# One transfer instead of two for the row of maxima of two attention heads, with both heads' low parts of Q in the same 64 partitions

## Chip, cores and metric

The kernel runs on one core of one Trainium2 chip. The metric is the device time of one execution in microseconds; the time given is the median of several executions. The profile is one execution recorded by the hardware profiler.

## The reference

The input x has 4 sequences of 1024 tokens with 128 features, all in float32. Four lines carry what matters here: attention over 16 heads of 64 features, with a causal mask and a softmax, and a layer norm behind it.

```
q, k, v = einsum('BSE,EHK->BSHK', x, w_q / w_k / w_v)          # 16 heads, K = 64
probs   = softmax(q k / sqrt(64) + causal mask, over the keys)
x       = layernorm(x + einsum('BSHK,EHK->BSE', probs v, w_o))
x       = layernorm(x + ffn(x))     # 128 -> 512, butterflies, gelu, butterflies, 512 -> 128
```

The softmax subtracts the maximum of each row of scores. The kernel must do this too, or get the same value in another way.

## The kernel before, in words

The attention is cut into 32 units (`UNITS`): 4 sequences times 8 pairs of heads. Each unit has 12 steps (`STEPS`); a step is one block of 128 keys against one chunk of up to 512 queries, and it is done for both heads of the pair.

**How a score is made.** TensorE works in fp32r, so Q and K are split in a high part (rounded) and a low part (the rest). A score is made by two matmuls into the same PSUM bank, in `scores`. The first (L671) multiplies `KHL` by `QH`: for head 0 the lower 64 partitions (0 to 63) of `KHL` hold K's high part and the upper 64 (64 to 127) its low part, and `QH` holds Q's high part in both halves; for head 1 the halves of `KHL` are swapped. The second (L675) multiplies `KH1` by `QL`. For head 0 the lower half of `KH1` holds a copy of K's high part and its upper half ones; the lower half of `QL` holds Q's low part, and its upper half zeros but for one row, partition 64 (`K`), which holds the negated maximum of each query. For head 1 it is the other way round: copy and low part above, ones and the row of maxima below, the row in partition 0. So the second matmul adds the low part's product and subtracts the maximum in one go, and ScalarE then only takes the exponential (L841).

**Where the row of maxima comes from.** During unit u, TensorE also does the work of unit u + 1 in the gaps ("fillers", laid out by hand in `FILL`): projections of Q and K (`proj`, L597 to L599), projections of V, and for the maxima the scores once more in one pass (`max`, L621). VectorE takes the maximum of each row (L966, L969) and then of the parts (L973). The last step of the chain is the filler `mt`, at step 10 between the two heads: TensorE transposes the maxima (L626), VectorE copies them to `NROW`, 16 rows of 128 numbers, 8 rows for each head (L979), and SyncE sends them to the rows of `QL` (`rows`, L392), with one transfer of 4 KB for each head. Each adds 16 to the semaphore `m_landed`. The second matmul of step 0, head 0, of the next unit (L675) waits until both have landed:

```
                    if s == 0 and h == 0:
                        pe.wait_ge(m_landed, (unit + 1) * 32)
```

**What else touches these tiles.** ScalarE rounds Q and K out of PSUM (`evacuate`, L778), one instruction for each head. VectorE subtracts the rounded part to make the low part (`lo`, L890, called in `consume`). SyncE copies Q's high part to the other half of `QH` (L378), and K's high part from `KHL` to `KH1` (L382), one transfer for each head and chunk; `dup_landed` counts them, and the first `max` filler of each chunk waits for it. `QL` is double-buffered (`par`), so a row of unit u + 1 goes to another buffer than the one that unit u reads. The zeros of `QL` are set once by VectorE (L893, L894), the ones of `KH1` once by GpSimd (L453, L455).

**The order on SyncE's queue.** In each unit: the copies of the next unit (`copies`), the three transfers of the inverted sums of the unit before (`inverses`), then the rows (`rows`), and in some units one 512 KB load of butterfly weights (`stage_weights`, L360). SyncE waits in this order, so nothing overtakes.

Of the kernel before, what the change touches and what calls it, by code (L numbers as in the profile page):

```python
# [24 lines left out]
F32 = mybir.dt.float32  # L25
# [3 lines left out]
P = 128  # L29
B, S, D = 4, 1024, 128  # L30
H, K = 16, 64
# [157 lines left out]
def post_norm_layer(nc, x, w_q, w_k, w_v, w_o, W_exp, b_exp, up_w, up_b, down_w, W_con, b_con, down_b, out):  # L189
    ctx = ExitStack()  # L190
    with ctx:
# [153 lines left out]
        @block.sync  # L345
        def _(sp):
            sp.dma_start(X[:, 0:TILES, :], x_tiles[:, 0:TILES, :]).then_inc(in_x[0], 16)
            for n, w in enumerate((w_q, w_k, w_v)):
                sp.dma_start(WQKV[:, n, :], w.rearrange("e h k -> e (h k)")).then_inc(in_w, 16)
            sp.dma_start(BLOCKS, b_exp.rearrange("(a n) -> a n", a=HT)).then_inc(in_b, 16)  # L350
            sp.dma_start(up_b_row, up_b.rearrange("(a n) -> a n", a=1)).then_inc(in_b, 16)
            sp.dma_start(W1[:, :], W_exp).then_inc(in_exp, 16)

            def stage_weights(n):

                if n > 0:
                    sp.wait_ge(composed, 3 * n)
                w, st = (up_w, n) if n < STAGES else (down_w, 2 * STAGES - 1 - n)
                src = w[st:st + 1].rearrange("a k i o -> a (k i o)").broadcast_to([P, 2 * HID])
                sp.dma_start(SW[:, :], src).then_inc(stage_in, 16)  # L360

            for st in range(STAGES):
                w = up_w[st:st + 1].rearrange("s k i o -> s (k i o)")
                if st < BLOCK_STAGES:
                    sp.dma_start(inner_w[st], w.rearrange("s (a n) -> (s a) n", a=HT)).then_inc(in_rows, 16)
                else:
                    sp.dma_start(outer_w[st - BLOCK_STAGES], w).then_inc(in_rows, 16)
            sp.dma_start(X[:, TILES:, :], x_tiles[:, TILES:, :]).then_inc(in_x[1], 16)

            def copies(unit):  # L370

                par = unit % 2
                A, Bh = slice(0, K), slice(K, P)
                for c in range(CHUNKS):
                    cols = slice(c * CH, (c + 1) * CH)
                    sp.wait_ge(qk_hi, (unit * 2 * CHUNKS + (2 * c + 1)))
                    for h, src, dst in ((0, A, Bh), (1, Bh, A)):
                        sp.dma_start(QH[dst, par, h, cols].bitcast(F32), QH[src, par, h, cols].bitcast(F32))\  # L378
                            .then_inc(dup_landed[c], 16)
                    sp.wait_ge(qk_hi, (unit * 2 * CHUNKS + (2 * c + 2)))  # L380
                    for h, half in ((0, A), (1, Bh)):
                        sp.dma_start(KH1[half, par, h, cols].bitcast(F32), KHL[half, par, h, cols].bitcast(F32))\  # L382
                            .then_inc(dup_landed[c], 16)

            def rows(unit):

                par = unit % 2
                sp.wait_ge(nrow_made, (unit + 1))
                for h in range(2):
                    row = K if h == 0 else 0  # L390
                    dst = QL[row:row + 1, par, h, :].rearrange("a (t c) -> a t c", t=TILES)
                    sp.dma_start(dst.bitcast(F32), NROW[h * TILES:(h + 1) * TILES, :].bitcast(F32)).then_inc(m_landed, 16)  # L392


            def inverses(unit):

                sp.wait_ge(sums_out, unit + 1)
                sp.dma_start(RCOL[:, 0, :], R0[0:P:P // 4, :].rearrange("a (p e) -> a p e", p=P // 4)).then_inc(sums_landed, 16)
                sp.wait_ge(recip_made, unit + 1)
                sp.wait_ge(o_free, unit * CHUNKS + O_CREDIT)  # L400
                sp.dma_start(RROW.rearrange("h (p e) -> (h p) e", p=K), RCOL[:, 1, :]).then_inc(recip_landed, 16)
                sp.wait_ge(recip_landed, unit * 16 + 16)
                for h in range(2):
                    sp.dma_start(R[h * K:(h + 1) * K, :, :].rearrange("p q c -> p (q c)"),
                                 RROW[h:h + 1, :].broadcast_to([K, CHUNKS * CH])).then_inc(inverse_landed, 16)

            copies(0)
            sp.sem_inc(sums_landed, 16)
            sp.wait_ge(blocks_done, 1)
            sp.dma_start(BROW, BLOCKS).then_inc(brow_in, 16)  # L410
            sp.dma_start(wo_nat, w_o.rearrange("e h k -> e (h k)")).then_inc(in_wo, 16)
            sp.dma_start(wcon_nat, W_con.rearrange("(t p) d -> p t d", p=P)).then_inc(in_con, 16)
            sp.dma_start(BC[:, :], b_con.rearrange("(a n) -> a n", a=1).broadcast_to([P, D])).then_inc(in_bc, 16)
            sp.dma_start(down_row, down_b.rearrange("(a n) -> a n", a=1).broadcast_to([P, D])).then_inc(in_bc, 16)
            rows(0)
            for u in range(UNITS):
                if u + 1 < UNITS:
                    copies(u + 1)
                if u > 0:
                    inverses(u - 1)  # L420
                if u + 1 < UNITS:
                    rows(u + 1)
                for n in range(2 * STAGES):
                    if STAGE_UNIT[n] - 1 == u:
                        stage_weights(n)
            inverses(UNITS - 1)
            sp.wait_ge(m_landed, 32 * UNITS)
            for c in range(CHUNKS):
                sp.wait_ge(dup_landed[c], 64 * UNITS)

            for g in range(B * CHUNKS):
                sp.wait_ge(out_made, (g + 1) * TPC)
                sp.dma_start(out_tiles[:, g * TPC:(g + 1) * TPC, :],
                             X[:, g * TPC:(g + 1) * TPC, :]).then_inc(out_stored, 16)
            sp.wait_ge(out_stored, 16 * B * CHUNKS)
# [3 lines left out]
        def _(pool):  # L439
# [10 lines left out]
            nc.gpsimd.memset(HALF[:], -0.5).then_inc(half_set, 1)  # L450

            pool.wait_ge(half_set, 1)
            nc.gpsimd.memset(KH1[K:P, :, 0, :].bitcast(F32), 1.0).then_inc(ones_rows_set, 1)  # L453
            pool.wait_ge(ones_rows_set, 1)
            nc.gpsimd.memset(KH1[0:K, :, 1, :].bitcast(F32), 1.0).then_inc(ones_rows_set, 1)  # L455
            pool.wait_ge(ones_rows_set, 2)
            pool.sem_inc(add_done, ADD_CREDIT)
            pool_n = 2

# [96 lines left out]
        def _(pe):  # L556
# [105 lines left out]
            def scores(unit, s):  # L662
                qc, kt = STEPS[s]
                par = unit % 2
                q0, n = qc * CH + START[s], CH - START[s]
                for h in range(2):
                    use = 2 * s + h
                    dst = SC[use % NSC][:, 0:n]

                    pe.wait_ge(exp_done, unit * 2 * NS + use + 1)  # L670
                    nc.tensor.matmul(dst, KHL[:, par, h, kt * P:(kt + 1) * P], QH[:, par, h, q0:q0 + n],  # L671
                                     start=True, stop=False)
                    if s == 0 and h == 0:
                        pe.wait_ge(m_landed, (unit + 1) * 32)
                    nc.tensor.matmul(dst, KH1[:, par, h, kt * P:(kt + 1) * P], QL[:, par, h, q0:q0 + n],  # L675
                                     start=False, stop=True).then_inc(scores_ready, 1)
                    if h == 0:
                        fill(unit, s, BETWEEN)
# [42 lines left out]
                t = nc.tensor.matmul(lay_banks[len(LAY) % 4][:, i:i + 1], BROW[:, i * P:(i + 1) * P], ONES[0:1, 0:1],  # L721
                                     start=True, stop=True)
            t.then_inc(laid_made, 1)
            pe.wait_ge(ones_rows_set, 2)
            pe.wait_ge(laid_copied, len(LAY) + 1)
            for u in range(UNITS):
                window(u)
# [152 lines left out]
        def _(dve):  # L880
# [8 lines left out]
            def lo(dst, src, hi_part):  # L889
                return nc.vector.tensor_tensor(dst, src, hi_part.bitcast(F32), ALU.subtract)  # L890


            nc.vector.memset(QL[K:P, :, 0, :].bitcast(F32), 0.0)  # L893
            nc.vector.memset(QL[0:K, :, 1, :].bitcast(F32), 0.0)  # L894
            nc.vector.memset(NEGM[:], 0.0)
            nc.vector.memset(MP[:], LOWEST).then_inc(rows_set, 1)

# [37 lines left out]
            def consume(u, f, at):  # L935
# [3 lines left out]
                if f[0] == "proj":  # L939
# [7 lines left out]
                    A, Bh = slice(0, K), slice(K, P)  # L947
                    if n == 0:
                        lo(QL[A, nxt, 0, cols], w[A, :], QH[A, nxt, 0, cols])
                        op = lo(QL[Bh, nxt, 1, cols], w[Bh, :], QH[Bh, nxt, 1, cols])  # L950
                    else:
                        lo(KHL[Bh, nxt, 0, cols], w[A, :], KHL[A, nxt, 0, cols])
                        op = lo(KHL[A, nxt, 1, cols], w[Bh, :], KHL[Bh, nxt, 1, cols])
# [21 lines left out]
                elif f[0] == "mt":  # L975
                    dve.wait_ge(work_ready, at + 1)
                    if u >= 0:
                        dve.wait_ge(m_landed, (u + 1) * 32)
                    nc.vector.tensor_copy(NROW[:, :], w[0:2 * TILES, 0:P]).then_inc(nrow_made, 1)  # L979
                    dve.wait_ge(nrow_made, u + 2)  # L980
                    dve.sem_inc(free, 1)
# [160 lines left out]
```

## Time and profile before

| | us |
|---|---|
| median of 3 executions | 1057.71 |
| lowest and highest | 1055.47, 1058.67 |
| the profiled execution, its own time | 1057.07 |
| its span, first to last instruction | 1054.7 |

In the profile PE is TensorE's matmuls, PEld its weight loads, DVE VectorE, ACT ScalarE, POOL GpSimd and SPq the queue of SyncE that issues transfers. L675 is line 675 of the kernel. Matmuls are pipelined, and their ends are modelled; two matmul rows may overlap. A wait is inferred from the semaphores: the profile names the engine or transfer that came last. Times in the timeline count from the start of the span.

### The profile page before, as it was taken

The page shows a single profiled execution, that of the slowest core. Times are in us where ns is not written, and L with a number is a line of the kernel's source. Part 1 is how long each engine was busy: PE and PEld are TensorE (multiplying, and loading weights), DVE is VectorE, ACT ScalarE, POOL GpSimd, SP SyncE. Part 2 cuts the span into 40 slices and gives each one's busy share as a digit, 9 for nine tenths or more (in the row PEclk, how much of TensorE's full clock was granted, in tenths as well). Part 3 has the DMA queues.
Part 4 walks back from the last instruction along what each step waited for, and adds up shares of the span by engine and source line. Part 5 has one row for each costly group of instructions (what it writes and reads, how often), then busy time and mean ns, then how long its engine had stood idle before and what let it go on. Part 6 is the DMA issues. An engine that isn't in the chain of part 4 may idle for free.

```text
span 1054.7 us, 17699 instructions
## 1 busy us (share of the span) xinstructions
PE 1016.9 (96%) x5816; PEld 697.3 (66%) x5816; DVE 754.2 (72%) x2014; ACT 602.9 (57%) x1214; POOL 757.4 (72%) x726
## 2 busy tenths in 40 slices
PE   4799999999999999999999999999999999999997
PEld 3556666676666666767666766766666676675576
DVE  6666777777677778777778777776778778873456
ACT  4355566665565566666656556666656656664431
POOL 6278776777779777777779877777778987777322
PEclk9699999999999999999999999999999999999998
DMA  7112223232231223232231222332222222320002
GB/s 221 45 46 66 56 57 82 62 81 75 48 81 38 65 62 82 62 81 62 62 81 47 66 53 61 81 81 62 72 52 81 63 51 53 80 62 21 21 18 64
DMA packets 45800, 68.69 MB, mean 65 GB/s; under 512 B 15079, under 2 KB 21515, under 8 KB 45710
## 3 DMA queue, kind: packets, MB, share of 16 engines
q1 hardware_dynamic: 45710, 67.57, 25.2%
q8 instruction: 47, 0.77, 0.3%
q14 instruction: 43, 0.35, 0.1%
HBM read 31.11 MB, written 2.36 MB: 32 GB/s over the span
## 4 chain that ended last, share of the span: by engine, by line
PE 86%; DMA 6%; POOL 3%; DVE 2%; issue 2%; SPq 1%; ACT 0%; POOLq 0%; DVEq 0%; ACTq 0%
PE O L696 24%; PE WORK L621 13%; PE SC L671 12%; PE SC L675 12%; PE WORK L636 4%; PE WORK L658 3%; PE WORK L758 3%; PE WORK L599 3%; PE WORK L598 3%; PE WORK L597 3%; DMA QL<-NROW 2%; DMA R<-RROW 2%; PE SC L746 1%; PE WORK L746 1%; PE WORK L607 1%
## 5 line engine op out<-in xcount | busy, mean ns | idle before, releaser
L841 ACT ACTIVATE PR<-SC 128x512 f32<-128x512 f32 (+3 forms) x768 | 355.0, 490 | 283.4 <-PE SC L675 247.3
L498 POOL TENSOR_TENSOR SUM<-SUM,PR 128x1024 f32<-128x1024 f32 (+3 forms) x256 | 419.1, 1637 | 14.0
L966 DVE CUSTOM_DVE_ANT_0 WORK<-WORK,CMASK 128x128 f32<-128x128 f32 (+3 forms) x512 | 239.4, 514 | 65.0 <-PE WORK L621 65.0
L671 PE MATMUL SC<-QH,KHL 128*128 128x512 f32 (+3 forms) x768 | 272.0, 359 | 4.8 <-ACT PR L841 3.2
L675 PE MATMUL SC<-QL,KH 128*128 128x512 f32 (+3 forms) x768 | 263.9, 347 | 3.1 <-DMA QL<-NROW 3.0
L483 POOL TENSOR_SCALAR_AFFINE_SELECT PR<-PR 128x256 f32<-128x256 f32 x256 | 105.7, 414 | 213.1 <-ACT PR L841 212.9
L621 PE MATMUL WORK<-KHL,QH 128*128 128x512 f32 (+3 forms) x768 | 224.8, 361 | 5.1 <-DMA KH<-KHL 3.7
L696 PE MATMUL O<-PR,VLO 128*64 128x512 f32 (+3 forms) x1024 | 200.0, 522 | 2.0 <-DVE OT L1036 1.9
L671 PEld LDWEIGHTS SC<-QH,KHL 128*128 128x128 f32 x768 | 145.3, 189 | 63.3 <-ACT PR L841 29.2
L621 PEld LDWEIGHTS WORK<-KHL,QH 128*128 128x128 f32 x768 | 135.5, 190 | 55.8 <-issue 34.9
L969 DVE TENSOR_REDUCE MP<-WORK 128x1 f32<-128x512 f32 x256 | 164.3, 685 | 4.6
L675 PEld LDWEIGHTS SC<-QL,KH 128*128 128x128 f32 x768 | 145.5, 189 | 16.3 <-DMA QL<-NROW 5.9
L890 DVE TENSOR_TENSOR QL<-WORK,QH 64x512 fp32r<-64x512 f32 x128 | 88.1, 688 | 78.6 <-ACT QH L778 77.6
L507 POOL TENSOR_TENSOR SUM<-PR 128x768 f32<-128x768 f32 x64 | 136.3, 2130 | 1.4 <-ACT PR L841 1.4
L696 PEld LDWEIGHTS O<-PR,VLO 128*64 128x64 f32 x1024 | 64.9, 136 | 106.3 <-issue 78.4
L890 DVE TENSOR_TENSOR KHL<-WORK,KHL 64x512 fp32r<-64x512 f32 x128 | 88.1, 688 | 43.2 <-ACT KHL L778 41.1
L778 ACT ACTIVATE QH<-WORK 64x512 fp32r<-64x512 f32 x128 | 75.6, 590 | 28.6 <-PE WORK L599 27.8
L778 ACT ACTIVATE KHL<-WORK 64x512 fp32r<-64x512 f32 x128 | 75.9, 593 | 4.7 <-PE WORK L599 1.4
L696 PE MATMUL O<-PR,VHI 128*64 128x256 f32 (+3 forms) x512 | 74.3, 432 | 0.0
L966 DVE DVE_READ_ACCUMULATOR2_ANT MP<- 128x1 f32 x512 | 72.7, 142 | 0.0
L696 PEld LDWEIGHTS O<-PR,VHI 128*64 128x64 f32 x512 | 36.8, 137 | 52.6 <-issue 46.8
L636 PE MATMUL WORK<-WOT,OT 128*128 128x128 f32 x512 | 63.7, 278 | 0.0
(102 smaller groups left out, 1070.9 us busy)
## 6 DMA issues: line engine op xcount, KB each, us to landing
QH<-QH SPq DMA_DIRECT2D x128, 128.0 KB, 2.3
KH<-KHL SPq DMA_DIRECT2D x128, 128.0 KB, 2.3
R<-RROW SPq DMA_DIRECT2D x64, 256.0 KB, 3.9
SW<-in_L_ffn_up_weights_dram SPq DMA_DIRECT2D x9, 512.0 KB, 4.7
SW<-_L_ffn_down_weights_dram SPq DMA_DIRECT2D x9, 512.0 KB, 4.8
out_dram<-X SPq DMA_DIRECT2D x8, 256.0 KB, 2.3
QL<-NROW SPq DMA_DIRECT2D x64, 4.0 KB
X<-in_L_attn_x_BSE_dram SPq DMA_DIRECT2D x1, 512.0 KB, 4.3
```

The costliest lines, as they stand in the source:

```text
L498: nc.gpsimd.tensor_tensor(total, total, prob(unit, s), ALU.add).then_inc(add_done, 1)
L507: nc.gpsimd.tensor_tensor(total, first[:, :, START[s]:], prob(unit, s), ALU.add).then_inc(add_done, 1)
L621: t = nc.tensor.matmul(w[:, at_col:at_col + n], QH[:, nxt, h, qt * P:(qt + 1) * P], KHL[:, nxt, h, lo:lo + n], start=True, stop=True)
L636: t = nc.tensor.matmul(w[:, k * P:(k + 1) * P], attended(pair, qc)[:, k * P:(k + 1) * P], WOT[:, pair % PAIRS, :], start=pair < last, stop ...
L671: nc.tensor.matmul(dst, KHL[:, par, h, kt * P:(kt + 1) * P], QH[:, par, h, q0:q0 + n], start=True, stop=False)
L675: nc.tensor.matmul(dst, KH1[:, par, h, kt * P:(kt + 1) * P], QL[:, par, h, q0:q0 + n], start=False, stop=True).then_inc(scores_ready, 1)
L696: t = nc.tensor.matmul(O[qc][h * K:(h + 1) * K, START[s]:], values(unit, kt)[:, h * K:(h + 1) * K], p[:, h, :], start=kt == 0, stop=s == L ...
L778: return nc.scalar.activation(dst, src, ACT.Copy)
L841: nc.scalar.activation(prob(unit, s)[:, h, :], SC[use % NSC][:, 0:n], ACT.Exp, scale=K ** -0.5).then_inc(exp_done, 1)
L890: return nc.vector.tensor_tensor(dst, src, hi_part.bitcast(F32), ALU.subtract)
L966: op = nc.vector.tensor_tensor_reduce(cols, cols, CMASK[:, CH - n:], 1.0, LOWEST, ALU.add, ALU.max, cell)
L969: op = nc.vector.tensor_reduce(cell, cols, AX_X, ALU.max)
```

## The change

Both heads now have the same layout in the second matmul: the low part of Q and the copy of K's high part lie in partitions 0 to 63, ones and the row of maxima in partitions 64 to 127, the row in partition 64. Both rows then lie one behind the other in one partition, and one transfer of 8 KB carries both. VectorE's subtraction for head 1 reads partitions 64 to 127 and writes 0 to 63; SyncE's copy of K's high part for head 1 goes from the upper to the lower half.

```diff
                     for h, half in ((0, A), (1, Bh)):
-                        sp.dma_start(KH1[half, par, h, cols].bitcast(F32), KHL[half, par, h, cols].bitcast(F32))\
+                        sp.dma_start(KH1[A, par, h, cols].bitcast(F32), KHL[half, par, h, cols].bitcast(F32))\
                             .then_inc(dup_landed[c], 16)
...
                 sp.wait_ge(nrow_made, (unit + 1))
-                for h in range(2):
-                    row = K if h == 0 else 0
-                    dst = QL[row:row + 1, par, h, :].rearrange("a (t c) -> a t c", t=TILES)
-                    sp.dma_start(dst.bitcast(F32), NROW[h * TILES:(h + 1) * TILES, :].bitcast(F32)).then_inc(m_landed, 16)
-
+                dst = QL[K:K + 1, par, :, :].rearrange("a h (t c) -> a (h t) c", t=TILES)
+                sp.dma_start(dst.bitcast(F32), NROW[:, :].bitcast(F32)).then_inc(m_landed, 16)
...
-            nc.gpsimd.memset(KH1[K:P, :, 0, :].bitcast(F32), 1.0).then_inc(ones_rows_set, 1)
+            nc.gpsimd.memset(KH1[K:P, :, :, :].bitcast(F32), 1.0).then_inc(ones_rows_set, 1)
             pool.wait_ge(ones_rows_set, 1)
-            nc.gpsimd.memset(KH1[0:K, :, 1, :].bitcast(F32), 1.0).then_inc(ones_rows_set, 1)
-            pool.wait_ge(ones_rows_set, 2)
...
                     if s == 0 and h == 0:
-                        pe.wait_ge(m_landed, (unit + 1) * 32)
+                        pe.wait_ge(m_landed, (unit + 1) * 16)
...
-            nc.vector.memset(QL[K:P, :, 0, :].bitcast(F32), 0.0)
-            nc.vector.memset(QL[0:K, :, 1, :].bitcast(F32), 0.0)
+            nc.vector.memset(QL[K:P, :, :, :].bitcast(F32), 0.0)
...
                         lo(QL[A, nxt, 0, cols], w[A, :], QH[A, nxt, 0, cols])
-                        op = lo(QL[Bh, nxt, 1, cols], w[Bh, :], QH[Bh, nxt, 1, cols])
+                        op = lo(QL[A, nxt, 1, cols], w[Bh, :], QH[Bh, nxt, 1, cols])
...
                     if u >= 0:
-                        dve.wait_ge(m_landed, (u + 1) * 32)
+                        dve.wait_ge(m_landed, (u + 1) * 16)
```

The other waits on `m_landed` (SyncE's at the end) and on `ones_rows_set` (TensorE's before the first unit) count 16 and 1 in place of 32 and 2.

## Rows read from the trace of the kernel before

**Rows 1.** The page: busy time of each engine.
```profile
PE 1016.9 (96%) x5816; PEld 697.3 (66%) x5816; DVE 754.2 (72%) x2014; ACT 602.9 (57%) x1214; POOL 757.4 (72%) x726
```
**Rows 2.** The chain of waits that ended last, by engine (the page).
```profile
PE 86%; DMA 6%; POOL 3%; DVE 2%; issue 2%; SPq 1%; ACT 0%; POOLq 0%; DVEq 0%; ACTq 0%
```
**Rows 3.** Waits over the whole span: who waited for what, us in total, times, longest.
```profile
PEld SC L675 <- DMA QL<-NROW: 5.9, 9, 1.3
...
PE SC L675 <- DMA QL<-NROW: 3.0, 6, 0.9
```
**Rows 4.** Timeline at a boundary of units without a wait (start, length, what).
```profile
275.13 1.43 SPq L392 DMA_DIRECT2D QL<-NROW  x2
...
276.98 1.18 SPq L378 DMA_DIRECT2D QH<-QH  x2
...
277.80 0.19 PEld L675 LDWEIGHTS SC<-QL,KH 128*128 128x128 f32 x1
```
**Rows 5.** Chain in order of time at a boundary with a wait.
```profile
334.07 0.70 SPq L392
334.82 3.10 DMA QL<-NROW
337.97 0.51 PE SC L675
```
**Rows 6.** Windows of two units in turn: length, busy times, PEclk, DMA share, GB/s.
```profile
304.70:334.05 29.35, 29.35 (x173) 20.19 (x172) 22.53 (x64) 18.18 (x38) 22.00 (x21) 1.00 0.27 73
334.05:364.54 30.49, 29.66 (x173) 20.18 (x172) 22.72 (x65) 18.38 (x39) 24.02 (x23) 1.00 0.23 54
```
**Rows 7.** Timeline: the three longest of the nine waiting weight loads (bracket: idle before).
```profile
161.29 0.19 PEld L675 LDWEIGHTS SC<-QL,KH 128*128 128x128 f32 x1 [1.25 <-DMA QL<-NROW]
...
337.96 0.19 PEld L675 LDWEIGHTS SC<-QL,KH 128*128 128x128 f32 x1 [1.15 <-DMA QL<-NROW]
...
721.01 0.19 PEld L675 LDWEIGHTS SC<-QL,KH 128*128 128x128 f32 x1 [0.69 <-DMA QL<-NROW]
```
**Rows 8.** Transfers between 277 and 278 us, in 40 slices of 0.025 us.
```profile
GB/s 0 0 0 0 0 0 0 0 82 42 41 0 0 0 0 0 0 0 0 0 0 0 0 0 0 0 0 0 0 0 0 0 0 0 0 0 0 0 0 0
```
**Rows 9.** Transfers between 335 and 337 us, in 40 slices of 0.05 us, and by queue.
```profile
GB/s 0 0 0 0 0 0 0 0 389 11 0 0 0 0 0 0 0 0 0 0 0 0 31 31 10 0 0 0 0 0 10 10 0 0 0 0 0 0 0 0
...
q8 instruction: 1, 0.02, 3.5%
```
**Rows 10.** Transfers between 571.5 and 573 us, in 40 slices of 0.0375 us, and by queue.
```profile
GB/s 0 0 0 0 0 0 0 0 0 0 0 0 55 55 437 0 0 0 0 0 0 0 0 0 0 0 0 0 0 0 0 14 68 28 0 0 0 0 0 0
...
q8 instruction: 1, 0.02, 3.9%
```
**Rows 11.** Timeline: the weight load that follows the transfers of rows 10.
```profile
573.29 0.19 PEld L675 LDWEIGHTS SC<-QL,KH 128*128 128x128 f32 x1
```
**Rows 12.** Groups by line: busy, mean ns of one, idle before.
```profile
L890 DVE TENSOR_TENSOR QL<-WORK,QH 64x512 fp32r<-64x512 f32 x128 | 88.1, 688 | 78.6 <-ACT QH L778 77.6
L890 DVE TENSOR_TENSOR KHL<-WORK,KHL 64x512 fp32r<-64x512 f32 x128 | 88.1, 688 | 43.2 <-ACT KHL L778 41.1
```
**Rows 13.** Issues of transfers: count, KB, median us to landing (the page).
```profile
QH<-QH SPq DMA_DIRECT2D x128, 128.0 KB, 2.3
KH<-KHL SPq DMA_DIRECT2D x128, 128.0 KB, 2.3
R<-RROW SPq DMA_DIRECT2D x64, 256.0 KB, 3.9
```
**Rows 14.** Timeline from the issue of K's copies to the first maxima of the next unit.
```profile
280.84 1.10 SPq L382 DMA_DIRECT2D KH<-KHL  x2
...
285.74 0.30 PEld L621 LDWEIGHTS WORK<-KHL,QH 128*128 128x128 f32 x2 [0.84 <-issue]
```
**Rows 15.** Timeline of the start: the first row and the first unit.
```profile
38.14 1.34 SPq L392 DMA_DIRECT2D QL<-NROW  x2
...
42.36 0.77 PE L671 MATMUL SC<-QH,KHL 128*128 128x512 f32 x1 [1.48 <-issue]
```

More of the change, by code:

```diff
@@ L426, in _ @@
             inverses(UNITS - 1)
-            sp.wait_ge(m_landed, 32 * UNITS)
+            sp.wait_ge(m_landed, 16 * UNITS)
             for c in range(CHUNKS):
@@ L723, in _ @@
             t.then_inc(laid_made, 1)
-            pe.wait_ge(ones_rows_set, 2)
+            pe.wait_ge(ones_rows_set, 1)
             pe.wait_ge(laid_copied, len(LAY) + 1)
```

## The prediction

> **What bounds the kernel now.** The page comes first: TensorE is busy 96% of the span, no other engine over 72% [rows 1]. The chain of waits says the same, PE 86% and DMA 6% [rows 2]. So only what gives TensorE time back counts. The waits over the whole span then say where it stands still: the weight load of the second matmul waited for the row of maxima 9 times, 5.9 us in all, 1.3 us at most. The matmul behind it shows 6 such waits, 3.0 us, which are the same stalls seen a second time and are not added [rows 3].
>
> There are 32 boundaries of units, and only 9 wait. The timeline shows why. At an ordinary one the two transfers are issued from 275.13 us on, in 1.43 us, and the weight load that needs them starts at 277.80 with no idle before it [rows 4]. So the row is there at most 2.67 us after the issue. When did it move? Between 277 and 278 us the bytes of the second transfer show at 277.20 to 277.27 [rows 8]: 2.07 us after the first issue. It landed between 2.07 and 2.67 us after it. The slack is between nothing and 0.60 us.
>
> At a boundary with a wait the first issue is at 334.07, the second at 334.82, and the matmul goes on at 337.97: the row took 3.10 us from the second issue, 3.85 from the first [rows 5]. In that stretch a 16 KB packet of the instruction queue starts in the same slice as the row's packets, 335.40, and a last piece of the row moves only from 336.50 on, when the others moved at 336.10 to 336.25 [rows 9]. My reading is that the fetch of instructions sits before one piece of the row in one DMA engine. It doesn't always hit: at 572.05 such a packet starts with the row's, the second set moves on time at 572.7, and the load at 573.29 has no wait [rows 10, 11].
>
> Does a wait lengthen the kernel by its full size? The unit with the wait of 1.15 us [rows 7] lasts 30.49 us, the one before it, with as many matmuls, 29.35 [rows 6]: 1.14 longer. Nothing downstream absorbs it. So the 5.9 us are the whole sum to be had.
>
> **The change part by part.**
> *The second issue goes.* The first transfer's issue takes 0.70 us and the second starts 0.75 after the first [rows 5]. One transfer carries all 16 rows of NROW, so the full row lands 0.75 us earlier if a transfer takes as long from its own issue: between 1.32 and 1.92 us after the issue. The slack grows to between 0.75 and 1.35 us. A delay that made a wait of up to 0.75 us now makes none. Of the nine, two are longer, 1.25 and 1.15 us; the third longest is 0.69 [rows 7]. The other seven, 5.9 - 1.25 - 1.15 = 3.5 us, vanish. The two leave 0.50 + 0.40 = 0.90 us, if the same fetch hits one transfer as it hit two; if the row is through before the fetch comes (it is out 0.75 earlier), they leave nothing. The gain is 5.0 to 5.9 us; I take the middle, 5.4.
>
> *Length of the issue and of the flight.* The bytes double in one transfer, 4 to 8 KB, all into one partition. The nearest rows bound the flight: the copies of 128 KB land 2.3 us after their issue, R's 256 KB 3.9 us [rows 13]. In the rows of before, 8 packets were moved within three slices of 0.025 us [rows 8], so 16 cost some 0.1 us more at most if they queue at one partition; I take 0 to 0.1, and the slack of 0.75 covers it. The issue may be a little cheaper: a pair of K's copies takes 1.10 us [rows 14] against 1.43 for a pair of rows [rows 4], 0.16 for one. Neither enters the sum, since an ordinary boundary has slack.
>
> The Trainium skill (DMA: Bandwidth & Descriptors, "Why a DMA increments its semaphore by 16 and not by 1") says that a transfer runs on the largest number of engines up to 16 that divides the slowest dimension of both sides: 8 for each of the old ones, 16 for the new, and that it counts as landed when all have finished. By that rule a fetch on any engine can hold up the row, where before half of them couldn't. The sum above would keep part of the waits; that is the first rival.
>
> *SyncE's queue.* It is free 0.7 us sooner behind the rows. Behind them stand the next copies of Q, issued at 276.98, 0.42 us after the rows' issue ended at 276.56 [rows 4]: they wait for ScalarE, not for the queue. Gain nothing. In the units with the 512 KB load, this starts earlier; it stood behind the rows before too.
>
> *VectorE.* The low part of Q of head 1 is now written across halves. The same instruction already crosses halves for K's low part: 688 ns for both, 64x512 each [rows 12]. Nothing, 0 to 0.
>
> *K's copy of head 1 crosses halves*, and both copies now write the lower one. The pair is issued from 280.84 on, in 1.10 us, so the second at about 281.39, and first used at 285.74 [rows 14]. With the 2.3 us to landing of both kinds of copy [rows 13] it is there at 283.7, 2.0 us early. Only if it took twice as long, 4.6 us, would it be late, by 0.3 us. Q's copies cross halves already, in both directions, and land in the same 2.3 us, so I take nothing.
>
> *Matmuls.* Same shapes, same counts, same number of zeros and ones. Nothing. *Memsets and start.* Two fills become one of the same size, on VectorE and on GpSimd, in the first microseconds; the first row, issued at 38.14 us, is needed only behind 42.36 [rows 15], so the start has slack for a later row too. Nothing. VectorE's `mt` waits for a transfer of a whole unit ago. Nothing.
>
> **Sum.** -5.4 us on the profiled execution: 1057.07 - 5.4 = 1051.7. The median shown is 0.64 above that execution, which gives 1052.3; between the two I say 1052.0. A measurement of this kernel can tell about 0.3%, 3.2 us, from no change, so the gain is a little above what can be seen.
>
> **The rivals.**
> *The fetch still hits.* With the row spread over more engines, other fetches get in its way. For it: all nine waits are tails, and the packet that missed at 572.05 may have been on an engine that the row didn't use. Against: only delays over 0.75 us still cost. If all nine became as long as the longest, each would leave 0.50: 4.5 us, a gain of 1.4, 1056.3. Same.
> *The time is given back.* TensorE comes earlier, and another engine is late at the boundary, or a fetch falls onto the copies instead. Against it is the comparison of two units above. Half the gain, 2.7 us: 1055.0, on the border.
> *Slower.* The single transfer lands later than the two did, in every unit: split over fewer engines because the two heads stay a dimension of two, or its 16 pieces queue at one partition. This would also be the change not doing what it says. It decides from 2.67 us after the issue [rows 4]; every 0.1 us beyond costs 32 x 0.1 = 3.2 us. At 2.9 us it is 7.4 us slower with the nine waits kept, 1065; as late as R's 3.9 [rows 13] it would be 39. Against it: the destination is one row without gaps, and 8 KB is a sixteenth of what lands in 2.3 us.
>
> **How the numbers follow.** The forecast has 0.65, the fetch 0.17, given back 0.12, slower 0.06. Faster by over 0.3%: the forecast and half of the third, 0.71; within 0.3%: 0.23; slower 0.06. The range reaches from the lowest run less the full 5.9 (1055.47 - 5.9 = 1049.6) to the first rival at 1056.3; it leaves out the slower case and some spread between executions.
>
> **What would show it.** One issue of rows in each unit, some 0.6 to 0.7 us; 32 in all. No wait of the second matmul's weight load for the row, or one or two under 0.6 us; units of 29.1 to 29.4 us where 30.49 stood. The prediction is wrong if these waits still sum to over 2 us, or if they are gone and the span hasn't shrunk by 4 us.

## The result, and the profile after

The changed kernel takes 1050.66 us (median of 9 executions, 1050.25 to 1052.58); the kernel before, measured with it, 1056.84 us (9 executions, 1054.45 to 1058.67). The ratio is 0.9935, with a 95% interval of 0.9922 to 0.9948: some 6.9 us less, between 5.5 and 8.2 (the two medians are 6.2 us apart). The profiled execution took 1050.42 us with a span of 1048.5, 6.2 us less than the span of before.

From the page of the kernel after, the line of busy times and that of the chain by engine:

```profile
PE 1014.8 (97%) x5816; PEld 697.7 (67%) x5816; DVE 753.1 (72%) x2013; ACT 602.8 (57%) x1214; POOL 757.2 (72%) x725
...
PE 91%; DMA 3%; DVE 2%; POOL 2%; issue 1%; SPq 1%; ACT 0%; POOLq 0%; DVEq 0%; ACTq 0%
```

TensorE has the same 5816 matmuls [rows 1], in a shorter span. In the chain the transfers' share went from 6% [rows 2] to 3%, and TensorE took it over: the row's transfer, 2% of the chain before by the page, is in it no more.

The view of the line that issues the row (L390, which was L392), kernel after. Its columns are the shortest, median and longest issue in ns, and the first and last start; then who waited for it, and the time from the start of an issue to landing:

```profile
L390 SPq DMA_DIRECT2D QL<-NROW x32: 547/552/575, 38.2 to 945.8; - x32
its engine sat idle before it (us, times) until:
who waited for it (us, times):
busy tenths in 40 slices 0000000000000000000000000000000000000000
DMA to landing us min/median/max: 1.8/1.8/1.8
```

Two things are to be seen. Nobody waited for the row, in any of the 32 units, where before there were 9 waits of 5.9 us in all [rows 3]. And the row never landed later than 1.8 us after its issue, where the longest of before needed nearly 4 from the first issue. The need is where it was at nearly all boundaries: 2.66 us after the issue. Here is the timeline of the kernel after at the boundary that stands in [rows 5], which lost 1.15 us before:

```profile
332.20 0.55 SPq L390 DMA_DIRECT2D QL<-NROW  x1
...
334.05 1.15 SPq L378 DMA_DIRECT2D QH<-QH  x2
334.75 0.19 PEld L666 LDWEIGHTS SC<-QH,KHL 128*128 128x128 f32 x1
...
334.86 0.19 PEld L670 LDWEIGHTS SC<-QL,KH 128*128 128x128 f32 x1
```

The last weight load starts 2.66 us after the issue (334.86 - 332.20), with no idle in a bracket. The windows of the two units that answer to [rows 6]:

```profile
302.85:332.20 29.35, 29.35 (x173) 20.16 (x172) 22.41 (x64) 18.17 (x38) 22.01 (x21) 1.00 0.27 73
332.20:361.57 29.37, 29.37 (x173) 20.20 (x172) 22.68 (x65) 18.36 (x39) 24.05 (x23) 1.00 0.23 56
```

The second was 30.49 us long and is 29.37: the 1.15 us of the wait, less 0.03, are back. The other lines that the change touches are as they were: the subtractions 688 ns for `QL` and 689 for `KHL`, K's copies 2.3 us to landing, each memset one of 3.5 us in place of two of 1.8.

### The profile page after: what moved, and what is told of

Its sections match the earlier page's. It is cut to its first block, busy times and chain, and to the rows that moved or that the text cites. A ratio compares the mean times of both kernels' runs of the same rounds, so it can differ in the third digit from the quotient of the medians.

```text
span 1048.5 us, 17665 instructions
## 1 busy us (share of the span) xinstructions
PE 1014.8 (97%) x5816; PEld 697.7 (67%) x5816; DVE 753.1 (72%) x2013; ACT 602.8 (57%) x1214; POOL 757.2 (72%) x725
## 3 DMA queue, kind: packets, MB, share of 16 engines
HBM read 31.11 MB, written 2.36 MB: 32 GB/s over the span
## 4 chain that ended last, share of the span: by engine, by line
PE 91%; DMA 3%; DVE 2%; POOL 2%; issue 1%; SPq 1%; ACT 0%; POOLq 0%; DVEq 0%; ACTq 0%
PE O L691 25%; PE WORK L616 14%; PE SC L666 13%; PE SC L670 12%; PE WORK L631 5%; PE WORK L653 3%; PE WORK L753 3%; PE WORK L594 3%; PE WORK L592 3%; PE WORK L593 3%; PE WORK L602 1%; PE WORK L604 1%; PE WORK L603 1%; PE SC L741 1%; PE WORK L741 1%; DMA R<-RROW 1%
```

## Experiments

Four questions were put. Does the gain come from the layout or from the transfer? Is it a matter of when the row lands against 2.66 us? Does the number of rows (and so of engines) in a transfer matter? Is it the delay or the extra traffic? The times below are ratios to the kernel before on the same chip. The kernels of the first four share one measurement, those of the last four another; in both the kernel before was at 1059 us.

### The new layout with two transfers

```diff
-                dst = QL[K:K + 1, par, :, :].rearrange("a h (t c) -> a (h t) c", t=TILES)
-                sp.dma_start(dst.bitcast(F32), NROW[:, :].bitcast(F32)).then_inc(m_landed, 16)
+                for h in range(2):
+                    dst = QL[K:K + 1, par, h, :].rearrange("a (t c) -> a t c", t=TILES)
+                    sp.dma_start(dst.bitcast(F32), NROW[h * TILES:(h + 1) * TILES, :].bitcast(F32)).then_inc(m_landed, 16)
```

The waits on `m_landed` count 32 for each unit again.

> The kernel after with its new layout, but with two transfers of 8 rows again, both into partition 64. Theory (the moment at which the whole row has landed is all that counts): two issues 0.75 us apart, the row whole at about 2.54 us after the first issue, against a need at 2.66; some 9 waits of the second matmul's weight load for the row, 4 to 7 us, and the time of the kernel before, 1056 to 1057.5 us. Rival 1 (the gain comes from the layout, the copies and subtractions that all go to the lower half): the gain stays, 1050 to 1052 us.

Measured: ratio 1.0001 (0.9986 to 1.0017), span 1053.9. The waits in its profile, us in total, times, longest:

```profile
PEld SC L671 <- DMA QL<-NROW: 5.4, 9, 1.3
```

Nine waits and 5.4 us, as before. Layout, subtractions, copies and memsets together are worth nothing that can be measured (the interval is some 1.6 us to either side). The whole gain is in how the row is sent.

### The old kernel with a semaphore for each head's row

```diff
-                    sp.dma_start(dst.bitcast(F32), NROW[h * TILES:(h + 1) * TILES, :].bitcast(F32)).then_inc(m_landed, 16)
+                    sp.dma_start(dst.bitcast(F32), NROW[h * TILES:(h + 1) * TILES, :].bitcast(F32)).then_inc(m_landed[h], 16)
...
-                    if s == 0 and h == 0:
-                        pe.wait_ge(m_landed, (unit + 1) * 32)
+                    if s == 0:
+                        pe.wait_ge(m_landed[h], (unit + 1) * 16)
```

VectorE and SyncE wait for both where they waited for 32.

> The kernel before, layout and both transfers unchanged, but each row has a semaphore of its own, and head 1's second matmul waits for head 1's row, head 0's only for its own. Theory: head 0's row lands 0.7 us before it is needed, head 1's is needed a good 0.46 us later than before (two matmuls of 0.23 us). Of the nine waits only their parts over 0.46 us stay: 0.1 + 0.8 + 0.7 + 0.15 + 0.2 + 0.2, some 2.1 us. Gain 3.8 us, about 1053 us. Rival 1 (layout): no gain, 1056 to 1057.5. Rival 2 (the gain comes from the number of engines that carry a transfer): no gain either.

Measured: ratio 0.9960 (0.9944 to 0.9975), some 4.2 us less, span 1052.6.

```profile
PEld O L697 <- DVE OT L1038: 13.9, 29, 1.8
PE O L697 <- DVE OT L1038: 2.9, 3, 1.3
...
PEld SC L676 <- DMA QL<-NROW: 2.3, 4, 0.8
```

The third line is the one that was forecast: 2.1 us expected, 2.3 found, in 4 waits. The sum came out, its parts did not: two of the four, 0.43 us at 102.13 and 0.82 at 894.41, are of head 0's load, which the theory had safe by 0.7 us; the two of head 1's load are 0.85 and 0.17. That the total agrees is partly luck. Still, waiting for each row only where it is needed brings more than half of the gain, without any change of layout. (The first two lines, waits for the inverted sums' transfers, vary from one execution to the next: 11.4 and 1.9 us in the trace of the kernel before. They hide part of this kernel's gain in the profiled span.)

### One and two transfers ahead of the row

```diff
+                for i in range(1):     # the other kernel: range(2)
+                    sp.dma_start(DUM[2 * TILES * i:2 * TILES * (i + 1), :], NROW[:, :].bitcast(F32)).then_inc(d_landed, 16)
                 dst = QL[K:K + 1, par, :, :].rearrange("a h (t c) -> a (h t) c", t=TILES)
```

`DUM` is a tile that nothing reads. SyncE waits for the unused transfers of the unit before ahead of issuing new ones, and VectorE waits for them too before it writes `NROW` again.

> The kernel after, with a second transfer of the same 16 rows into an unused tile issued ahead of the real one in each unit. The real row then lands about 0.6 us later, 2.4 us after the first issue, on 16 engines. Theory: ordinary boundaries still have 0.25 us to spare, but tails cost again, 1 to 5 us, 1052 to 1056 us. Rival 2 (a transfer that is spread over 16 engines isn't held up): no waits, 1050 to 1051.5 us.

> The kernel after, with two unused transfers of 16 rows ahead of the real one. Theory: the row lands about 3.0 us after the first issue, 0.3 to 0.4 us past the need, in each of the 31 or 32 units, 9 to 13 us of waits plus tails: 1060 to 1066 us. If the need at 2.66 us isn't where it decides, the time stays under 1056.

Measured: 1.0066 (1.0045 to 1.0087) with one ahead, span 1063.4; 1.0137 (1.0114 to 1.0159) with two, span 1072.4. Against the kernel after (span 1049.7 and 1048.5 in its two profiles) one ahead costs 14 to 15 us and two ahead 23 to 24; by the ratios (the kernel after has 0.9934 in the last group) it is 14 and 21.5. The wait of the weight load, first with one ahead, then with two:

```profile
PEld SC L677 <- DMA QL<-NROW: 13.5, 14, 1.4
```
```profile
PEld SC L677 <- DMA QL<-NROW: 21.8, 31, 1.6
```

With two ahead all but one of the boundaries wait, as the need at 2.66 us demands: the row's own issue starts 1.23 us after the first one (374.26 - 373.03), and with the 1.8 us to landing it is whole some 3.0 us after it. An ordinary boundary waits 0.37 us. At 31 boundaries that is 11.5 us; the other 10 us are tails. The expectation, 1060 to 1066 us, named the tails but made them too small: the median was 1073.6, with the kernel before at 1058.8. First issue, issue of the row, and the load that waits for it:

```profile
373.03 1.19 SPq L394 DMA_DIRECT2D DUM<-NROW  x2
374.26 0.59 SPq L396 DMA_DIRECT2D QL<-NROW  x1
...
376.14 0.19 PEld L677 LDWEIGHTS SC<-QL,KH 128*128 128x128 f32 x1 [0.37 <-DMA QL<-NROW]
```

One ahead is the surprise. The row is whole 2.4 us after the first issue at most boundaries, as expected, which is in time, yet 14 boundaries wait for 13.5 us in all, more than twice what the kernel before lost. The theory gave 1 to 5 us. It had the row's moment right and the frequency of tails wrong. One of the longest, in the timeline:

```profile
338.70 0.55 SPq L394 DMA_DIRECT2D DUM<-NROW  x1
...
339.29 0.59 SPq L396 DMA_DIRECT2D QL<-NROW  x1
...
342.85 0.19 PEld L677 LDWEIGHTS SC<-QL,KH 128*128 128x128 f32 x1 [1.41 <-DMA QL<-NROW]
```

And the bytes moved from 340 to 342 us in this kernel, in slices of 0.05 us:

```profile
GB/s 41 0 0 0 0 0 328 0 0 0 31 51 42 31 0 0 0 0 0 0 0 0 0 0 0 0 0 0 0 0 0 0 0 41 246 174 205 410 123 82
...
q8 instruction: 1, 0.02, 4.5%
```

The unused transfer's last pieces are in the first slice (340.0). The 16 KB fetch of instructions starts at 340.3. The row comes at 340.5 to 340.7, behind it, and is whole only shortly before 342.85. The bytes tell more: 31 + 51 + 42 + 31 GB/s over 0.05 us each are 7.75 KB, 15 pieces of 512 B. Of the 16 rows one is missing there and comes later. That is what one engine would do that is busy with the fetch; the fetch's share, 4.5% of 16 engines in 2 us, is 1.4 us of one engine.

Read boundary by boundary, the packets in this trace show 13 boundaries at which a fetch starts between 1.5 and 1.9 us after the first issue, behind the unused transfer's pieces (from 1.2 us on) and ahead of the row's (from 1.8). All 13 wait. The 14th wait, 0.21 us, has no fetch near it; see the part on the prediction.

### Eight rows: alone, and behind one transfer

The edit of the first; the second has in addition the unused transfer of 16 rows ahead of it, as above.

```diff
-                dst = QL[K:K + 1, par, :, :].rearrange("a h (t c) -> a (h t) c", t=TILES)
-                sp.dma_start(dst.bitcast(F32), NROW[:, :].bitcast(F32)).then_inc(m_landed, 16)
+                dst = QL[K:K + 1, par, 0, :].rearrange("a (t c) -> a t c", t=TILES)
+                sp.dma_start(dst.bitcast(F32), NROW[0:TILES, :].bitcast(F32)).then_inc(m_landed, 16)
```

> The kernel after, but the one transfer carries only the 8 rows of head 0; head 1's maxima are left out and its row stays zero, so that its exponentials are taken without a maximum subtracted. Theory (the moment of landing): issue 0.68 us as for the old transfers, landed 1.8 us after it, no wait for the row, the time of the kernel after, ratio to before 0.992 to 0.995. If the spread over 16 engines is what escapes the tails, the waits of before come back, 4 to 6 us, ratio 0.998 to 1.001.

> As the kernel with one unused transfer of 16 rows ahead (13.5 us of waits in 14 boundaries), but the real transfer carries only head 0's 8 rows, issued at the same moment; head 1's maxima are left out. Theory that a transfer on all engines meets each fetch of instructions, and one on half of them only half of the fetches: 5 to 8 boundaries with a wait, 5 to 9 us, 4 to 8 us faster than with 16 rows behind one (ratio to before 0.998 to 1.003). If only the moment counts and not the number of engines: 12 to 15 waits, 11 to 14 us, ratio 1.005 to 1.008.

Measured: eight rows alone 0.9943 (0.9928 to 0.9957), span 1050.9; behind one unused transfer 0.9959 (0.9944 to 0.9974), span 1053.9. First the line of the row's issue and its waits alone, then the same behind one:

```profile
L390 SPq DMA_DIRECT2D QL<-NROW x32: 667/700/712, 38.7 to 948.3; - x32
...
  PEld SC L670: 1.5, 2
```
```profile
L396 SPq DMA_DIRECT2D QL<-NROW x32: 691/700/709, 39.3 to 951.8; - x32
...
  PEld SC L677: 5.2, 7
```

Behind one, 7 boundaries wait where 14 did with 16 rows, and 5.2 us are lost in place of 13.5: half the hits, at the same moment of issue. The time fell by more than was expected: the ratio was to be 0.998 to 1.003, and the 11 us to the kernel with 16 rows behind one (1.0066, from the other measurement) are more than the 8.3 us of waits. Not every fetch between the two transfers hits any more: 12 boundaries have one there, and 7 of them wait, where it was 13 of 13. At 422.85 one starts, the row's packets follow at 423.10, and the load at 423.87 waits for nothing (slices of 0.05 us from 422):

```profile
GB/s 0 0 0 0 0 0 0 0 41 52 62 10 0 0 0 0 0 328 0 0 0 0 31 41 11 0 0 0 0 0 0 0 0 0 0 0 0 0 0 0
...
q8 instruction: 1, 0.02, 2.9%
```
```profile
423.87 0.19 PEld L677 LDWEIGHTS SC<-QL,KH 128*128 128x128 f32 x1
```

The row's three slices hold 4.15 KB (31 + 41 + 11 GB/s), all 8 pieces; none is missing. The same unit of the kernel with 16 rows behind one waits 0.95 us. This is what the Trainium skill's rule in DMA: Bandwidth & Descriptors ("Why a DMA increments its semaphore by 16 and not by 1") makes of it: 8 rows run on 8 engines, 16 rows on 16, and a transfer has landed when its slowest engine has. The traces agree in the share of fetches that hit, 13 of 13 against 7 of 12, and in the one piece that is missing after a hit; which engine carried a fetch, no view here shows. Eight rows are also half the bytes, and no run tells this from the number of engines.

Alone, the eight rows weren't free of waits as the theory had it: 2, of 1.5 us. At the longer one, 1.10 us, the fetch starts in the slice behind the first of the row's packets, 890.35 us (slices of 0.05 from 890):

```profile
GB/s 0 0 0 0 0 0 51 349 0 0 0 0 0 0 0 0 0 0 0 82 82 492 164 164 655 246 82 655 328 82 748 246 246 573 328 246 492 328 164 655
```

The slices at 890.30 and 890.35 hold 20 KB, the fetch's 16.4 and 7 pieces; again one is missing. So a single transfer is not safe by its early issue alone. The issue of 8 rows takes 0.70 us and that of 16 rows 0.55, and the packets of 8 rows start in the slice from 1.33 us after the start of the issue (890.30 - 888.97 at this boundary), those of 16 rows 1.2 (see below).

### The unused transfer behind the row, and the kernel after again

```diff
                 dst = QL[K:K + 1, par, :, :].rearrange("a h (t c) -> a (h t) c", t=TILES)
                 sp.dma_start(dst.bitcast(F32), NROW[:, :].bitcast(F32)).then_inc(m_landed, 16)
+                for i in range(1):
+                    sp.dma_start(DUM[2 * TILES * i:2 * TILES * (i + 1), :], NROW[:, :].bitcast(F32)).then_inc(d_landed, 16)
```

> The kernel after, with the unused transfer of 16 rows behind the real one instead of ahead of it: same traffic and same load of the queue as with one ahead, but the row isn't late. Theory: no wait for the row, the time of the kernel after, ratio to before 0.992 to 0.996. If the extra traffic or the queue made the loss, it is as slow as with one ahead, 1.005 to 1.008.

> The kernel after unchanged, on the same chip as the three beside it, as their measure: no wait for the row, ratio to before 0.992 to 0.995.

Measured: 0.9931 (0.9914 to 0.9947) with the unused transfer behind, 0.9934 (0.9920 to 0.9949) for the kernel after; both spans 1049.7, and neither profile has a wait for the row. The same bytes and the same time on SyncE's queue cost 14 us ahead of the row and nothing that can be measured behind it.

## Why the prediction was right

**The bound and the sum to be had.** Right. The 5.9 us of waits were all real time of TensorE; they are gone, and the span is 6.2 us shorter. The comparison of two units that stood for "nothing downstream absorbs it" holds in the kernel after: 30.49 to 29.37 us.

**The second issue goes.** Right. The row was to be whole 1.32 to 1.92 us after the issue; it is at 1.8. The seven short waits had to vanish and did. That it is the sending and not the layout is shown by the new layout with two transfers, ratio 1.0001.

One reading was off: the prediction took all nine waits for tails, and one of them is not, the load at 72.47 us.

```profile
72.47 0.19 PEld L675 LDWEIGHTS SC<-QL,KH 128*128 128x128 f32 x1 [0.21 <-DMA QL<-NROW]
```

The first issue is at 69.90, and no fetch starts near the row. The load starts 2.57 us after the issue, when elsewhere it would still be in time; here the need comes at 2.36 (2.57 - 0.21). The 14th wait of the kernel with one ahead is of this kind. The other eight have a fetch that starts between 1.3 and 2.1 us after the first issue; five more fetches start there and make no wait that the profile counts.

**The two long waits.** Mis-sized within the range: they were to leave 0 to 0.9 us, and I took the middle, 5.4 of 5.9 as gain. They left nothing. My reason for the upper end, that the row is out before the fetch comes, was the right one. At the boundary of [rows 5] the transfers of the kernel after, 333 to 335 us in slices of 0.05, are:

```profile
GB/s 0 0 0 0 0 0 0 0 62 52 52 0 0 0 0 328 0 0 0 0 0 0 0 0 0 0 0 0 0 0 0 0 0 0 0 0 0 0 0 0
...
q8 instruction: 1, 0.02, 3.3%
```

All 16 pieces move at 333.40 to 333.55, the fetch starts at 333.75. Before, it started in the slice of the first transfer's packets [rows 9], with the second transfer's still to come. There the bytes show 7 pieces beside the fetch, 7 at 336.10 to 336.25 and 2 at 336.50 to 336.60: one piece of each transfer was held up, where the prediction spoke of one. The fetch itself also came later than before, 1.55 us after the issue (333.75 - 332.20) against 1.33 (335.40 - 334.07), and in the two profiles of the kernel after none starts from the issue until 1.5 us behind it, when the row's last piece has moved, at 1.4. This the prediction did not foresee, and why it is so is open; so that nothing at all was left is partly luck.

**The rest of the gain.** 6.2 us of span against 5.9 of waits. The unit from 510.49 to 540.66 us of the kernel before was 30.17 us long, and in it TensorE waited 1.2 us for VectorE's scaling, which waited for the transfer of the inverted sums; its counterpart, without this wait, is 29.38. The kernel after has a wait of the same kind, 0.6 us, in another unit. These come and go between executions, and they are no effect of the change that these runs can show.

**The edits costed at nothing.** Right: the subtractions keep 688 ns, K's copies 2.3 us, and the start is the same, the first row being issued at 38.2 us against 38.1. The issue came out at 0.55 us, by which the sum doesn't change.

**The rivals.** *The fetch still hits* had the mechanism right: a transfer of 16 rows is exposed to twice as many fetches. With one transfer ahead it is what decides, 13 of 13 fetches against 7 of 12. It fell here because in the kernel after no fetch starts between the issue and the row's packets. I had priced such a hit on the kernel after and not asked when a fetch can start. *The time is given back* fell by the span, 6.2 us shorter for 5.9 us of waits. *Slower* fell by the landing, 1.8 us and never more; its turning point, 2.67 us, was right at nearly all boundaries, as the kernel with two transfers ahead shows.

## What to carry to other kernels

A semaphore that several small transfers fill is as late as the last one's worst case; on an engine that is busy 96% of the time it is enough that a few boundaries in 32 miss. So measure the distance from issue to need at each boundary and look at the tails, not at the median: here the ordinary boundary was in time by 0.1 us, nine others cost 6 us, and a transfer of 8 KB put ahead of the one that matters cost 14. What is needed first goes first on its queue and in one piece; where a merge isn't possible, a semaphore for each piece, waited for where it is needed, gave 4.2 of the 6.9 us here.

## What the runs showed of the hardware that was not expected

- A fetch of instructions that gets ahead of a small transfer holds up one piece of it for about as long as it keeps its engine: 1.1 us in [rows 9] (3.5% of 16 engines in 2 us), 1.4 us with one ahead. But the landing comes later still. In [rows 9] the row's last piece moved some 0.3 us late, and the row was whole 1.3 us late, 1.3 us behind that piece; in the kernel after 0.4 to 0.5 us lie between the last piece and the landing. What fills the rest is open.
- A transfer of 16 rows of 512 B takes less time to issue than one of 8: 0.55 us against 0.70. It lands 1.8 us after its issue; for 8 rows the views give no landing, but the load at 72.47 us that waited for them starts 1.84 us after the start of their issue.
- With 16 rows in a single transfer the fetches near the row started behind its packets, not among them; with 8 rows one started among them (890.35 us), and with a second transfer of 16 rows they came between the two. They do not come more often there: in the kernel after, too, 12 of the 32 boundaries have a fetch between 1.5 and 2.0 us after the issue, when the row's pieces have moved. What sets this moment is open. No run tried it.
